# Moving the sums of squares of k and q in an attention stage from VectorE to ScalarE

## The chip, the cores and the metric

The kernel runs on one core of a Trainium2 chip. The metric is the device time of one execution in microseconds. The core's engines are called PE (TensorE), DVE (VectorE), ACT (ScalarE), POOL (GpSimd) and SP (SyncE, which here only issues DMAs). They run side by side and meet only at semaphores.

## The reference, cut to what matters

The kernel computes two layers, each an attention and a feed-forward part. The change concerns the second attention alone. There q and k are normalised per head before the scores:

```
def rms_norm(x, w):
    var = jnp.mean(jnp.square(x.astype(jnp.float32)), axis=-1, keepdims=True)
    return (x * jax.lax.rsqrt(var + EPS)).astype(x.dtype) * w
...
kv = jnp.concatenate([context, latents], axis=1)     # 64 + 256 keys
q, k, v = ...                                        # 32 heads of q, 8 of k and v, 128 wide
q = rms_norm(q, q_norm_w); k = rms_norm(k, k_norm_w)
scores = jnp.einsum('bhgqd,bhkd->bhgqk', qg, k) * scale
out = einsum(softmax(scores), v) @ Wo
```

The sum of squares over the 128 elements of a head is what moves to another engine.

## The kernel before, in words

The second attention (`attn1_phase`) runs 32 units: 8 groups g (a k/v head and its four q heads) times 4 batches b, so unit n = 4g + b. Group 0 and group 7 are written out, groups 1 to 6 are a hardware loop. Each engine has its own program (`body`), and its order is written out by hand. All matrix products are made of three passes over a high and a low part of each operand (`mm3`, lines 55 to 57): ACT copies a PSUM bank to the high part, DVE then subtracts to get the low part. Each unit is software-pipelined: while unit n makes its k, v, q and scores, the engines turn the probabilities of unit n-1 (`turn`, lines 1224 and 1229), multiply them with v (`p_v`, 1243), and project (`out`).

What one unit does, in the order of PE:

- k and v products (`kv`), and for even b also the context's (`cx`);
- turns j = 0 and 1 of unit n-1, the q product of token tile 0, whose last of four chunks waits for the low part of turn 0; turns 2 and 3 (turn 3 waits for the low part of turn 1), the q product of tile 1, turns 4 and 5 (turn 4 waits for the low part of turn 3);
- `p_v` of head pair 0; the transposes of k (L1314), which reuse the PSUM bank of turn 4 and so wait for its low part; the transposes of q, tile 0 (L1323), which wait likewise for turn 5; `p_v` of head pair 1; the transposes of q, tile 1, which wait for the low part of kT;
- scores 0 and 1, out 0, scores 2, out 1, scores 3.

What ACT does beside it: copies of k and v (L1142 to L1149), then for j = 0 to 5 the high part of turn j (`t_evac`, L1126 and L1129), with the copy of q tile 0 after j = 1 and of tile 1 after j = 3 (L1159), the high part of `p_v` 0 (`pv_evac`, L1134) after j = 5, then kT (L1163, L1166), qT (L1171), and the four pairs of exponentials (L1183, with row sums as accumulated outputs).

DVE makes the low parts (`t_lo` L962 and L966, `pv_lo` L972, kT_lo L1058, qT_lo L1068), the sums of squares of k (L1031: 3 for even b, 2 for odd) between the low parts of turns 0 and 1, those of q (`q_squares`, L986: four per tile) after the low parts of turns 3 and 5, the scaling of k (L1044), the row maxima and their scaled negatives (L993, L997), the reciprocals and scaling of p (L1003, L1008). POOL turns the sums of squares into reciprocal roots (rk L923 and L925, rq L931 and L933), scales a quarter of p (L916), and makes the low parts of the weights: of `o` in unit b = 1 right behind rk, of `kv` and `q` in unit b = 3 (L909, four or two pieces of 128x512). k cannot be turned before DVE has scaled it, and the exponentials need rq.

Of the kernel before, what the change touches and what calls it, by code (L numbers as in the profile page):

```python
# [23 lines left out]
ALU = mybir.AluOpType  # L24
# [8 lines left out]
HD = 128  # L33
NKV = 8
GH = 4
# [780 lines left out]
def attn1_phase(nc, k, sem, ln):  # L816


    def sems(*names):
        return [sem("a1_" + n) for n in names]  # L820
# [7 lines left out]
        "t_full", "t_hi", "t_split", "kt_full", "kt_hi", "kt_split", "qt_full", "qt_hi", "qt_split")  # L828
    ssk_ready, rk_ms, rk_ready, k_scaled, ssq_ready, rq_ms, rq_ready = sems(
# [61 lines left out]
    with nc.Block() as block:  # L891
# [60 lines left out]
        def _(dve):  # L952
# [29 lines left out]
            def q_squares(n, b, tile):  # L982
                dve.wait_ge(q_copied, 2 * n + tile + 1)
                for h in range(GH):
                    q = k.q_raw[:, tile, h * HD:(h + 1) * HD]
                    last = dve.tensor_tensor_reduce(k.dump[:, tile * GH + h, :], q, q, 1.0, 0.0, ALU.mult, ALU.add,  # L986
                                                    k.ssq[:, tile * GH + h:tile * GH + h + 1])
                if tile == 1:
                    last.then_inc(ssq_ready, 1)

# [21 lines left out]
            def body(g, first, nxt):  # L1012
                for b in range(BATCH):
# [16 lines left out]
                    for i in range(nk):  # L1030
                        last = dve.tensor_tensor_reduce(k.dump[:, 2 * GH + i, :], k.k_raw[:, i, :], k.k_raw[:, i, :], 1.0, 0.0,  # L1031
                                                        ALU.mult, ALU.add, k.ssk[:, i:i + 1])
                    last.then_inc(ssk_ready, 1)
# [15 lines left out]
                    q_squares(n, b, 0)  # L1049
# [3 lines left out]
                    q_squares(n, b, 1)  # L1053
# [62 lines left out]
            dve.wait_ge(stats_set, 1)  # L1116
# [3 lines left out]
        def _(act):  # L1120
# [15 lines left out]

            def body(g, first, nxt):
                for b in range(BATCH):
                    n, prev = BATCH * g + b, not (first and b == 0)
                    act.wait_ge(kv_full, n + 1)  # L1140
                    bank = y_bank(b, "kv")[:, :].rearrange("p (t n) -> p t n", t=2)
                    act.activation(k.k_raw[:, 0:2, :], bank[:, :, 0:HD], ACT.Copy)  # L1142
                    act.activation(k.v[0][:, b, 0:2, :], bank[:, :, HD:2 * HD], ACT.Copy).then_inc(kv_hi, 1)
                    if b % 2 == 0:
                        act.wait_ge(cx_full, 2 * g + b // 2 + 1)
                        act.activation(k.k_raw[:, 2, :], y_bank(b, "cx")[:, 0:HD], ACT.Copy)
# [4 lines left out]
                        last.then_inc(cx_hi, 1)  # L1151
                    for j in range(6):
                        if prev:
                            t_evac(n, b, j)
                            if j == 5:
                                pv_evac(n, b, 0)
                        if j in (1, 3):
                            act.wait_ge(q_full, 2 * n + j // 2 + 1)
                            act.activation(k.q_raw[:, j // 2, :], y_bank(b, "q", j // 2)[:, :], ACT.Copy)\  # L1159
                               .then_inc(q_copied, 1)  # L1160
                    act.wait_ge(kt_full, n + 1)
# [39 lines left out]

            loop(act, body, tail)
# [486 lines left out]
```

## Time and profile before

| | us |
|---|---|
| median of 3 runs | 1532.51 (1532.06 to 1532.99) |
| profiled execution | 1530.52 |
| its span | 1528.7 |
| PE busy | 1427.2 (93%) |
| DVE busy | 1136.9 (74%) |
| ACT busy | 756.8 (50%) |
| POOL busy | 519.6 (34%) |

The span is the time from the first to the last instruction of the profiled execution; 1.8 us lie around it. The first copy of k (L1142) starts at 583.9 us and the last at 1424.2, which places the second attention: it is some 58% of the span. The granted TensorE clock is full in all of it. Busy time of PE is modelled, because matmuls overlap: the start of one to the start of the next is the better measure.

### The profile page before, as it was taken

The page shows a single profiled execution, that of the slowest core. Times are in us where ns is not written, and L with a number is a line of the kernel's source. Part 1 is how long each engine was busy: PE and PEld are TensorE (multiplying, and loading weights), DVE is VectorE, ACT ScalarE, POOL GpSimd, SP SyncE. Part 2 cuts the span into 40 slices and gives each one's busy share as a digit, 9 for nine tenths or more (in the row PEclk, how much of TensorE's full clock was granted, in tenths as well). Part 3 has the DMA queues.
Part 4 walks back from the last instruction along what each step waited for, and adds up shares of the span by engine and source line. Part 5 has one row for each costly group of instructions (what it writes and reads, how often), then busy time and mean ns, then how long its engine had stood idle before and what let it go on. Part 6 is the DMA issues. An engine that isn't in the chain of part 4 may idle for free. (4 is left out here: it accounts for less than half of the span.)

```text
span 1528.7 us, 24378 instructions
## 1 busy us (share of the span) xinstructions
PE 1427.2 (93%) x8064; PEld 1209.9 (79%) x8064; DVE 1136.9 (74%) x2870; ACT 756.8 (50%) x2127; POOL 519.6 (34%) x586
## 2 busy tenths in 40 slices
PE   5999999999999998999999999999999999999879
PEld 4888888887778887787888878878878887877767
DVE  7888888888651426778778788787787787787765
ACT  5666666667220314545544545555545545455531
POOL 5733333443691822232132133132132223322220
PEclk9999999999999999999999999999999999999999
DMA  4111111220230400100101001001001001000001
GB/s 186 70 67 44 69 55 69 69 69 1 83 112 28 136 13 0 70 1 6 65 1 68 1 0 69 0 0 69 0 0 69 0 0 69 14 29 13 1 1 55
DMA packets 14933, 63.75 MB, mean 42 GB/s; under 512 B 1760, under 2 KB 1760, under 8 KB 10656
## 3 DMA queue, kind: packets, MB, share of 16 engines
q1 hardware_dynamic: 14880, 63.07, 11.6%
q8 instruction: 30, 0.49, 0.1%
q14 instruction: 23, 0.19, 0.0%
HBM read 60.97 MB, written 2.10 MB: 41 GB/s over the span
## 5 line engine op out<-in xcount | busy, mean ns | idle before, releaser
L1183 ACT ACTIVATE p<-psum,nb,rq 128x320 f32<-128x320 f32 x256 | 155.4, 614 | 208.4 <-DVE nb L997 208.3
L55 PE MATMUL psum<-w1q_hi,xnT_lo 128*128 128x512 f32 x256 | 107.8, 421 | 7.9 <-DVE v_lo L1017 4.3
L993 DVE TENSOR_REDUCE mx<-psum 128x2 f32<-128x640 f32 x128 | 105.0, 820 | 9.3 <-PE psum L57 3.8
L923 POOL TENSOR_TENSOR rk<-ssk,rms_eps 128x3 f32<-128x3 f32 x32 | 6.3, 196 | 299.7 <-DVE ssk L1031 299.7
L962 DVE TENSOR_TENSOR pT_lo<-psum,pT_hi 128x512 fp32r<-128x512 f32 x128 | 87.9, 687 | 23.4 <-ACT pT_hi L1126 21.4
L243 POOL TENSOR_TENSOR p<-p,rinv 128x256 f32<-128x256 f32 x64 | 39.3, 614 | 192.0 <-DVE rinv L319 192.0
L434 ACT ACTIVATE p<-psum,nb 128x64 f32<-128x64 f32 x256 | 76.8, 313 | 51.0 <-DVE nb L344 50.9
L57 PE MATMUL psum<-w1q_hi,xnT_hi 128*128 128x512 f32 x256 | 100.6, 393 | 0.0
L55 PE MATMUL psum<-w1o_hi,oT_lo 128*128 128x512 f32 x256 | 100.4, 392 | 0.0
L56 PE MATMUL psum<-w1o_lo,oT_hi 128*128 128x512 f32 x256 | 100.3, 392 | 0.0
L56 PE MATMUL psum<-w1q_lo,xnT_hi 128*128 128x512 f32 x256 | 99.8, 390 | 0.0
L57 PE MATMUL psum<-w1o_hi,oT_hi 128*128 128x512 f32 x256 | 99.8, 390 | 0.0
L313 DVE TENSOR_TENSOR VW_lo<-psum,VW_hi 64x512 fp32r<-64x512 f32 x128 | 88.0, 687 | 13.5 <-ACT VW_hi L419 11.6
L1159 ACT ACTIVATE q_raw<-psum 128x512 f32<-128x512 f32 x64 | 38.2, 598 | 117.6 <-PE psum L57 117.6
L1229 PE MATMUL psum<-ident,p 128*128 128x128 f32 x512 | 73.2, 276 | 21.8 <-DVE pT_lo L962 13.7
L419 ACT ACTIVATE VW_hi<-psum 64x512 fp32r<-64x512 f32 x128 | 75.8, 592 | 22.9 <-PE psum L57 21.4
L55 PE MATMUL psum<-kT_hi,qT_lo 128*128 128x320 f32 x256 | 83.4, 326 | 3.2 <-ACT p L1183 2.3
L55 PE MATMUL psum<-w_kv_hi,xnT_lo 128*128 128x256 f32 x288 | 82.3, 286 | 3.1 <-PEq L642 1.8
L1229 PEld LDWEIGHTS psum<-ident,p 128*128 128x128 f32 x512 | 57.6, 140 | 34.1 <-DVE pT_lo L962 17.7
L1008 DVE TENSOR_SCALAR p<-p,rinv 128x320 f32<-128x320 f32 x192 | 80.4, 461 | 3.4
L57 PE MATMUL psum<-w_kv_hi,xnT_hi 128*128 128x256 f32 x288 | 82.2, 285 | 0.0
L56 PE MATMUL psum<-w_kv_lo,xnT_hi 128*128 128x256 f32 x288 | 82.2, 285 | 0.0
(249 smaller groups left out, 4821.8 us busy)
## 6 DMA issues: line engine op xcount, KB each, us to landing
raw_q<-in_w0q SPq DMA_DIRECT2D x8, 1024.0 KB, 4.9
raw_o<-in_w0o SPq DMA_DIRECT2D x8, 1024.0 KB, 4.8
raw_q<-in_w1q SPq DMA_DIRECT2D x8, 1024.0 KB, 7.5
raw_o<-in_w1o SPq DMA_DIRECT2D x8, 1024.0 KB, 4.8
raw_kv<-in_w_gu SPq DMA_DIRECT2D x10, 512.0 KB, 3.5
raw_gu<-in_w_gu SPq DMA_DIRECT2D x10, 512.0 KB, 3.6
raw_kv<-in_w0kv SPq DMA_DIRECT2D x8, 515.0 KB, 3.3
raw_kv<-in_w1kv SPq DMA_DIRECT2D x8, 512.0 KB, 5.5
```

The costliest lines, as they stand in the source:

```text
L55: pe.matmul(out, w[1], m[0], start=start, stop=False)
L56: pe.matmul(out, w[0], m[1], start=False, stop=False)
L57: return pe.matmul(out, w[0], m[0], start=False, stop=stop)
L243: pool.tensor_tensor(p, p, spread(k.rinv0[:, t % 4, :]), ALU.mult).then_inc(p_ready, 1)
L313: last = dve.tensor_tensor(k.VW[1][r, h // 2, 2 * pr + bp, :], bank[64 * bp:64 * bp + 64, :], f(k.VW[0][r, h // 2, 2 * pr + bp, :]), ALU.s ...
L419: last = act.activation(k.VW[0][r, h // 2, 2 * pr + bp, :], bank[64 * bp:64 * bp + 64, :], ACT.Copy)
L434: last = act.activation(k.p0[:, s % 4, h * CTX:(h + 1) * CTX], s_bank[s % 2][:, h * CTX:(h + 1) * CTX], ACT.Exp, scale=SCALE, bias=k.nb0[: ...
L962: last = dve.tensor_tensor(k.pT[1][:, kt, 2 * hp:2 * hp + 2, :], bank.rearrange("p (h q) -> p h q", h=2), f(k.pT[0][:, kt, 2 * hp:2 * hp + ...
L993: dve.tensor_reduce(k.mx[:, stat(j)], s_pair(j), AX.X, ALU.max).then_inc(mx_ready, 1)
L1008: last = dve.tensor_scalar(k.p1[:, tile, h, :], k.p1[:, tile, h, :], k.rinv[:, tile * GH + h:tile * GH + h + 1], None, ALU.mult)
L1183: last = act.activation(k.p1[:, tile, h, :], s_pair(j)[:, h % 2, :], ACT.Exp, bias=k.nb[:, i:i + 1], scale=k.rq[:, i:i + 1], accum_out=k.r ...
L1229: last = pe.transpose(bank[:, (2 * hh + tile) * PART:(2 * hh + tile + 1) * PART], k.p1[:, tile, 2 * hp + hh, CTX * hh + kt * PART:CTX * hh ...
```

## The change

Both kinds of sums of squares leave DVE. ACT makes each by one square with an accumulated output into the same `ssk` and `ssq` columns. The squares of k come right behind the copies of k and v (and, in even units, of the context's), ahead of the high part of turn 0. The four of q tile 0 come between the high part of turn 3 and the copy of q tile 1; two of tile 1 right behind that copy, ahead of turn 4; the other two between turn 5 and `p_v` 0. A new semaphore tells ACT that its own copy of k is written; before the squares of q it waits on `q_copied` in the same way. The wait for the first memset of POOL moves from DVE to ACT.

```
--- before.py
+++ after.py
@@ -826,6 +826,7 @@
         "q_full", "q_copied", "pv_full", "pv_hi", "pv_split", "d_full", "x_added")
     t_full, t_hi, t_split, kt_full, kt_hi, kt_split, qt_full, qt_hi, qt_split = sems(
         "t_full", "t_hi", "t_split", "kt_full", "kt_hi", "kt_split", "qt_full", "qt_hi", "qt_split")
+    k_copied = sem("a1_k_copied")
     ssk_ready, rk_ms, rk_ready, k_scaled, ssq_ready, rq_ms, rq_ready = sems(
         "ssk", "rk_ms", "rk", "k_scaled", "ssq", "rq_ms", "rq")
     s_full, mx_ready, nb_ready, exp_done, rinv_ready, p_scaled, stats_set, p_scaled_pool = sems(
@@ -979,15 +980,6 @@
                 dve.scalar_tensor_tensor(out=k.x[:, t, :], in0=y_bank(b, "d", j)[:, :], scalar=k.gate[:, 1:2],
                                          in1=k.x[:, t, :], op0=ALU.mult, op1=ALU.add).then_inc(x_added, 1)
 
-            def q_squares(n, b, tile):
-                dve.wait_ge(q_copied, 2 * n + tile + 1)
-                for h in range(GH):
-                    q = k.q_raw[:, tile, h * HD:(h + 1) * HD]
-                    last = dve.tensor_tensor_reduce(k.dump[:, tile * GH + h, :], q, q, 1.0, 0.0, ALU.mult, ALU.add,
-                                                    k.ssq[:, tile * GH + h:tile * GH + h + 1])
-                if tile == 1:
-                    last.then_inc(ssq_ready, 1)
-
             def row_max(n, j):
                 dve.wait_ge(s_full, 4 * n + j + 1)
                 dve.tensor_reduce(k.mx[:, stat(j)], s_pair(j), AX.X, ALU.max).then_inc(mx_ready, 1)
@@ -1027,10 +1019,6 @@
                     if prev:
                         t_lo(n, b, 0)
                     nk = 3 if b % 2 == 0 else 2
-                    for i in range(nk):
-                        last = dve.tensor_tensor_reduce(k.dump[:, 2 * GH + i, :], k.k_raw[:, i, :], k.k_raw[:, i, :], 1.0, 0.0,
-                                                        ALU.mult, ALU.add, k.ssk[:, i:i + 1])
-                    last.then_inc(ssk_ready, 1)
                     if not nxt and b >= 2:
                         ln.dve_stats(dve, 3, 2 * b - 4)
                         ln.dve_stats(dve, 3, 2 * b - 3)
@@ -1046,11 +1034,9 @@
                     if prev:
                         t_lo(n, b, 2)
                         t_lo(n, b, 3)
-                    q_squares(n, b, 0)
                     if prev:
                         t_lo(n, b, 4)
                         t_lo(n, b, 5)
-                    q_squares(n, b, 1)
                     if prev:
                         pv_lo(n, b, 0)
                     dve.wait_ge(kt_hi, n + 1)
@@ -1113,7 +1099,6 @@
 
             w_hi("q", 0)
             own_lo("q")
-            dve.wait_ge(stats_set, 1)
             loop(dve, body, tail)
 
         @block.scalar
@@ -1134,30 +1119,56 @@
                 act.activation(k.oT[0][:, 2 * hp:2 * hp + 2, :],
                                y_bank(b, "pv", hp)[:, :].rearrange("p (h q) -> p h q", h=2), ACT.Copy).then_inc(pv_hi, 1)
 
+            def k_squares(n, nk):
+                act.wait_ge(k_copied, n + 1)
+                for i in range(nk):
+                    last = act.activation(k.dump[:, 2 * GH + i, :], k.k_raw[:, i, :], ACT.Square,
+                                          accum_out=k.ssk[:, i:i + 1])
+                last.then_inc(ssk_ready, 1)
+
+            def q_squares(n, tile, heads):
+                act.wait_ge(q_copied, 2 * n + tile + 1)
+                for h in heads:
+                    i = tile * GH + h
+                    last = act.activation(k.dump[:, i, :], k.q_raw[:, tile, h * HD:(h + 1) * HD], ACT.Square,
+                                          accum_out=k.ssq[:, i:i + 1])
+                if i == 2 * GH - 1:
+                    last.then_inc(ssq_ready, 1)
+
             def body(g, first, nxt):
                 for b in range(BATCH):
                     n, prev = BATCH * g + b, not (first and b == 0)
+                    nk = 3 if b % 2 == 0 else 2
                     act.wait_ge(kv_full, n + 1)
                     bank = y_bank(b, "kv")[:, :].rearrange("p (t n) -> p t n", t=2)
-                    act.activation(k.k_raw[:, 0:2, :], bank[:, :, 0:HD], ACT.Copy)
+                    last = act.activation(k.k_raw[:, 0:2, :], bank[:, :, 0:HD], ACT.Copy)
+                    if nk == 2:
+                        last.then_inc(k_copied, 1)
                     act.activation(k.v[0][:, b, 0:2, :], bank[:, :, HD:2 * HD], ACT.Copy).then_inc(kv_hi, 1)
                     if b % 2 == 0:
                         act.wait_ge(cx_full, 2 * g + b // 2 + 1)
-                        act.activation(k.k_raw[:, 2, :], y_bank(b, "cx")[:, 0:HD], ACT.Copy)
+                        act.activation(k.k_raw[:, 2, :], y_bank(b, "cx")[:, 0:HD], ACT.Copy).then_inc(k_copied, 1)
                         for i in range(2):
                             for half in (slice(0, 64), slice(64, PART)):
                                 last = act.activation(k.v[0][half, b + i, 2, :],
                                                       y_bank(b, "cx")[64 * i:64 * i + 64, HD:2 * HD], ACT.Copy)
                         last.then_inc(cx_hi, 1)
+                    k_squares(n, nk)
                     for j in range(6):
                         if prev:
                             t_evac(n, b, j)
-                            if j == 5:
-                                pv_evac(n, b, 0)
+                        if j == 3:
+                            q_squares(n, 0, range(GH))
                         if j in (1, 3):
                             act.wait_ge(q_full, 2 * n + j // 2 + 1)
                             act.activation(k.q_raw[:, j // 2, :], y_bank(b, "q", j // 2)[:, :], ACT.Copy)\
                                .then_inc(q_copied, 1)
+                        if j == 3:
+                            q_squares(n, 1, (0, 1))
+                        if j == 5:
+                            q_squares(n, 1, (2, 3))
+                            if prev:
+                                pv_evac(n, b, 0)
                     act.wait_ge(kt_full, n + 1)
                     bank = x_bank(b, "k")
                     last = act.activation(k.kT[0][:, b, CTX:KEYS], bank[:, 0:SEQ], ACT.Copy, scale=k.qkw[:, 0:1])
@@ -1199,6 +1210,7 @@
                 for t in (4, 5):
                     ln.act_hi(act, 3, t, ln_bank(4, t % 2))
 
+            act.wait_ge(stats_set, 1)
             loop(act, body, tail)
 
         @block.tensor
```

## Rows read from the trace of the kernel before

**Rows 1.** Busy time of each engine over four units, 850.26 to 958.89 us: sum and mean.
```profile
sum 108.63, PE 104.56 PEld 88.68 DVE 86.19 ACT 55.52 POOL 29.39; mean PE 26.14 PEld 22.17 DVE 21.55 ACT 13.88 POOL 7.35
```

**Rows 2.** One line's instructions: ns min/median/max, first and last start.
```profile
L986 DVE CUSTOM_DVE_ANT_0 dump<-q_raw x256: 279/285/1033, 590.7 to 1435.6; 128x128 f32<-128x128 f32 x128
```

**Rows 3.** ACT's groups by shape: out<-in, shapes, count | busy us, mean ns | idle before.
```profile
L1163 ACT ACTIVATE kT_hi<-psum,qkw 128x256 fp32r<-128x256 f32 x32 | 15.0, 468 | 0.0
L731 ACT ACTIVATE hT_hi<-f_h 128x512 fp32r<-128x512 f32 x20 | 12.7, 633 | 45.3 <-DVE f_h L705 45.3
L1142 ACT ACTIVATE k_raw<-psum 128x256 f32<-128x256 f32 x32 | 12.2, 382 | 25.2 <-PE psum L57 25.2
...
L444 ACT ACT_TABLE_LOAD x1 | 1.3, 1283 | 0.7 <-PEq L1679 0.7
```

**Rows 4.** Timeline of ACT, first attention: start us, us, instruction [idle before <-releaser].
```profile
202.16 0.30 ACT L434 ACTIVATE p<-psum,nb 128x64 f32<-128x64 f32 x1
...
202.45 0.31 ACT L434 ACTIVATE p<-psum,nb 128x64 f32<-128x64 f32 x1
```

**Rows 5.** Timeline of ACT, unit b=2 of a middle group.
```profile
853.00 1.08 ACT L1126 ACTIVATE pT_hi<-psum 128x512 fp32r<-128x512 f32 x2
...
859.66 0.60 ACT L1159 ACTIVATE q_raw<-psum 128x512 f32<-128x512 f32 x1 [1.81 <-PE psum L57]
860.15 0.59 ACT L1126 ACTIVATE pT_hi<-psum 128x512 fp32r<-128x512 f32 x1
```

**Rows 6.** Timeline of DVE, the same unit b=2.
```profile
854.24 0.69 DVE L962 TENSOR_TENSOR pT_lo<-psum,pT_hi 128x512 fp32r<-128x512 f32 x1
...
860.78 0.69 DVE L962 TENSOR_TENSOR pT_lo<-psum,pT_hi 128x512 fp32r<-128x512 f32 x1 [0.84 <-ACT pT_hi L1126]
```

**Rows 7.** Timeline of PE, the same unit b=2.
```profile
854.98 0.50 PE L55 MATMUL psum<-w1q_hi,xnT_lo 128*128 128x512 f32 x1 [0.38 <-DVE pT_lo L962]
...
862.42 0.66 PE L1323 MATMUL psum<-ident,q_raw 128*128 128x128 f32 x4
...
864.53 0.39 PE L1243 MATMUL psum<-pT_hi,v_hi 128*128 128x512 f32 x1
865.10 0.63 PE L1323 MATMUL psum<-ident,q_raw 128*128 128x128 f32 x4 [0.19 <-DVE kT_lo L1062]
865.79 0.41 PE L55 MATMUL psum<-kT_hi,qT_lo 128*128 128x320 f32 x1
```

**Rows 8.** Timeline of PE's weight loads, the same unit b=2.
```profile
856.22 0.42 PEld L1229 LDWEIGHTS psum<-ident,p 128*128 128x128 f32 x4 [0.29 <-DVE pT_lo L962]
```

**Rows 9.** Timeline of ACT, unit b=3 of the same group.
```profile
885.48 0.59 ACT L1126 ACTIVATE pT_hi<-psum 128x512 fp32r<-128x512 f32 x1
```

**Rows 10.** Timeline of PE, the same unit b=3.
```profile
887.74 0.66 PE L1323 MATMUL psum<-ident,q_raw 128*128 128x128 f32 x4
...
890.09 0.60 PE L1323 MATMUL psum<-ident,q_raw 128*128 128x128 f32 x4
890.60 0.41 PE L55 MATMUL psum<-kT_hi,qT_lo 128*128 128x320 f32 x1
```

**Rows 11.** Timeline of ACT, unit b=1 of the next group.
```profile
932.94 1.10 ACT L1126 ACTIVATE pT_hi<-psum 128x512 fp32r<-128x512 f32 x2
```

**Rows 12.** Timeline of POOL, the same unit b=1.
```profile
936.45 5.05 POOL L909 TENSOR_TENSOR w1o_lo<-raw_o,w1o_hi 128x512 fp32r<-128x512 f32 x4
```

**Rows 13.** Timeline of DVE, the same unit b=1.
```profile
936.52 2.58 DVE L1044 TENSOR_SCALAR k_raw<-k_raw,rk 128x128 f32<-128x128 f32 x2 [0.63 <-POOL rk L925]
```

**Rows 14.** Timeline of PE, the same unit b=1.
```profile
939.01 0.39 PE L57 MATMUL psum<-w1q_hi,xnT_hi 128*128 128x512 f32 x1
940.77 0.66 PE L1229 MATMUL psum<-ident,p 128*128 128x128 f32 x4 [1.37 <-DVE pT_lo L962]
...
943.85 0.66 PE L1323 MATMUL psum<-ident,q_raw 128*128 128x128 f32 x4
```

**Rows 15.** Timeline of ACT, the first unit of the stage.
```profile
591.50 0.47 ACT L1163 ACTIVATE kT_hi<-psum,qkw 128x256 fp32r<-128x256 f32 x1
```

More of the change, by code:

```diff
@@ L828, in attn1_phase @@
         "t_full", "t_hi", "t_split", "kt_full", "kt_hi", "kt_split", "qt_full", "qt_hi", "qt_split")
+    k_copied = sem("a1_k_copied")
     ssk_ready, rk_ms, rk_ready, k_scaled, ssq_ready, rq_ms, rq_ready = sems(
@@ L980, in x_add @@
                                          in1=k.x[:, t, :], op0=ALU.mult, op1=ALU.add).then_inc(x_added, 1)
[L982 to L989, printed above, removed]
             def row_max(n, j):
@@ L1029, in body @@
                     nk = 3 if b % 2 == 0 else 2
[L1030 to L1033, printed above, removed]
                     if not nxt and b >= 2:
@@ L1115, in _ @@
             own_lo("q")
-            dve.wait_ge(stats_set, 1)
             loop(dve, body, tail)
@@ L1135, in pv_evac, with k_squares, q_squares @@
                                y_bank(b, "pv", hp)[:, :].rearrange("p (h q) -> p h q", h=2), ACT.Copy).then_inc(pv_hi, 1)
+            def k_squares(n, nk):
+                act.wait_ge(k_copied, n + 1)
+                for i in range(nk):
+                    last = act.activation(k.dump[:, 2 * GH + i, :], k.k_raw[:, i, :], ACT.Square,
+                                          accum_out=k.ssk[:, i:i + 1])
+                last.then_inc(ssk_ready, 1)
+            def q_squares(n, tile, heads):
+                act.wait_ge(q_copied, 2 * n + tile + 1)
+                for h in heads:
+                    i = tile * GH + h
+                    last = act.activation(k.dump[:, i, :], k.q_raw[:, tile, h * HD:(h + 1) * HD], ACT.Square,
+                                          accum_out=k.ssq[:, i:i + 1])
+                if i == 2 * GH - 1:
+                    last.then_inc(ssq_ready, 1)
             def body(g, first, nxt):
@@ L1139, in body @@
                     n, prev = BATCH * g + b, not (first and b == 0)
+                    nk = 3 if b % 2 == 0 else 2
                     act.wait_ge(kv_full, n + 1)
                     bank = y_bank(b, "kv")[:, :].rearrange("p (t n) -> p t n", t=2)
-                    act.activation(k.k_raw[:, 0:2, :], bank[:, :, 0:HD], ACT.Copy)
+                    last = act.activation(k.k_raw[:, 0:2, :], bank[:, :, 0:HD], ACT.Copy)
+                    if nk == 2:
+                        last.then_inc(k_copied, 1)
                     act.activation(k.v[0][:, b, 0:2, :], bank[:, :, HD:2 * HD], ACT.Copy).then_inc(kv_hi, 1)
@@ L1145, in body @@
                         act.wait_ge(cx_full, 2 * g + b // 2 + 1)
-                        act.activation(k.k_raw[:, 2, :], y_bank(b, "cx")[:, 0:HD], ACT.Copy)
+                        act.activation(k.k_raw[:, 2, :], y_bank(b, "cx")[:, 0:HD], ACT.Copy).then_inc(k_copied, 1)
                         for i in range(2):
@@ L1151, in body @@
                         last.then_inc(cx_hi, 1)
+                    k_squares(n, nk)
                     for j in range(6):
@@ L1154, in body @@
                             t_evac(n, b, j)
-                            if j == 5:
-                                pv_evac(n, b, 0)
+                        if j == 3:
+                            q_squares(n, 0, range(GH))
                         if j in (1, 3):
@@ L1160, in body @@
                                .then_inc(q_copied, 1)
+                        if j == 3:
+                            q_squares(n, 1, (0, 1))
+                        if j == 5:
+                            q_squares(n, 1, (2, 3))
+                            if prev:
+                                pv_evac(n, b, 0)
                     act.wait_ge(kt_full, n + 1)
@@ L1200, in tail @@
                     ln.act_hi(act, 3, t, ln_bank(4, t % 2))
+            act.wait_ge(stats_set, 1)
             loop(act, body, tail)
```

2 lines of the change are left out of this document (removed).

## The prediction

> **What bounds the kernel now.** I read the windows first. In four units of the middle of the stage PE is busy 104.56 of 108.63 us, DVE 86.19, ACT 55.52 [rows 1]. So PE is the bound and everything else counts only where PE waits for it; a lighter DVE is worth nothing by itself. The timelines then show where PE waits, and the pattern repeats from group to group. In an even unit there are five places. The last chunk of the q product waits for the low part of turn 0 (0.38 us shown idle at 854.98) [rows 7]; turn 3 waits for that of turn 1 (0.29 on the weight loads) [rows 8]; the transposes of q tile 0 at 862.42 wait for turn 5; those of tile 1 at 865.10 wait for kT_lo; scores 0 at 865.79 wait for qT_lo [rows 7]. In unit b=1 there is one large wait: turn 4 starts at 940.77 instead of 939.24 (939.01 plus the 0.23 from one 512-column matmul to the next) because DVE is late with turn 3: 1.53 us [rows 14]. In b=3 the middle has only the wait of the q transposes for turn 5 [rows 10].
>
> The reader should see who sets the wait at turn 5. ACT starts the high part of turn 4 at 860.15, directly behind its copy of q tile 1 at 859.66 [rows 5]; DVE had been idle 0.84 us when it took that bank at 860.78 [rows 6]; PE gets the q transposes out at 862.42 [rows 7], 2.27 us after ACT's start. In b=3 the same distance is 885.48 to 887.74, 2.26 us [rows 9, 10]. So this point moves one to one with ACT's turn 4, and DVE's squares, which sit in DVE's idle time, do not matter for it. Two of the moved squares go exactly in front of it.
>
> **What goes.** 256 squares of q at a median of 0.285 us [rows 2] and 80 of k of the same form leave DVE, about 96 us of busy records, less in elapsed time because they overlap. Nearly all of it lies beside waits for ACT or POOL, so I cost the removal at nothing except in b=1 (below). The cover is DVE's own idle time, 0.84 us in row 860.78 alone [rows 6]; if it were gone, less DVE work could only help.
>
> **The price of a square on ACT.** No square with accumulation is in the trace. The nearest rows are the exponentials 128x64 with an accumulated output and one pointer operand: 0.29 us from start to start [rows 4]. Copies of 128x512 and 128x256 take 0.60 and 0.382 us [rows 3, 5], so 64 more columns cost 0.054. A pointer operand costs 0.468 - 0.382 = 0.086 [rows 3], and the square has none. A source in SBUF costs 0.633 - 0.60 = 0.033 more [rows 3, 5]. That gives 0.29 + 0.054 - 0.086 + 0.033 = 0.29 us each. Lower end 0.24 (the source free and a little less), upper end 0.40 (a pointer for the bias after all). I take 0.29, since the exponential differs from it only by terms that rows show. The wait of ACT for its own copy of q is new too: the copy is 0.60 long [rows 5], where the next instruction used to start after 0.49. I take 0.05 for the semaphore, between 0 and 0.15: 0.65 - 0.49 = 0.16 us.
>
> **Squares of k.** Three in an even unit move the high part of turn 0 from 853.00 to 853.87 [rows 5]. DVE needs 0.63 from there (860.15 to 860.78 [rows 5, 6]), so turn 0's low part starts at 854.50 instead of 854.24 [rows 6]: PE's wait grows by 0.26. Without DVE's three squares the low part of turn 1 comes directly behind, and the 0.29 at turn 3 goes: net -0.03. In odd units two squares cost 0.58, which by the same steps stays under PE's need: the low part of turn 0 is about 0.3 us early there. Nothing.
>
> **Squares of q.** Four of tile 0 (1.16 us) go into ACT's idle 1.81 before the copy of tile 1 [rows 5]: nothing, with 0.65 left, about 0.4 after the turns that now run later. Two of tile 1 and the wait, 0.58 + 0.16 = 0.74 us, push turn 4. Even unit: q transposes +0.74 - 0.03 = +0.71. Behind them p_v 1 now covers what tile 1 waited for: 865.10 less (864.53 + 0.23) = 0.34 [rows 7]. Scores 0 used to follow after 0.69 against 0.51 in b=3 [rows 7, 10]: 0.18 more. Net 0.71 - 0.34 - 0.18 = +0.19. In b=3 nothing waits behind the q transposes, so +0.74. The last two squares (0.58, ahead of p_v 0's high part) delay kT, but kT_lo is still some 0.3 us before PE's need, because DVE no longer makes its four squares in front of it. ssq is ready no later than before within about 0.3 us, and POOL's rq has over 2 us until the first exponential: nothing.
>
> **Unit b=1.** DVE's scaling of k takes 2.58 us for two small instructions, beside POOL's 5.05 us of w1o_lo that started 0.07 us earlier [rows 12, 13]; each scaling ends with a piece of POOL's (1.26 us). Behind it stands turn 3's low part, hence the 1.53. With the change ACT makes the k squares from 932.94 [rows 11], so rk is ready near 934.8 instead of 936.5. DVE reaches the scaling 0.63 (its wait for rk) and 0.43 (two squares) earlier, at 935.46. POOL has then already started at 934.8 and its pieces end near 936.0 and 937.3, so the second scaling ends near 937.4 instead of 939.1, and turn 3's low part 1.7 us earlier: the 1.53 goes whole. But then ACT's own order is the next thing late: the copy of q tile 1 at 939.43, plus 0.65 and 0.58, puts turn 4 at 940.66, and 2.27 later, at 942.93, come the q transposes instead of 943.85 [rows 14]. Net -0.92.
>
> What the Trainium skill says here (SBUF — State Buffer, section "SBUF: two separate sides"): DVE in a two-port mode and GpSimd take turns on one shared port pair, held for a whole instruction, while ACT never waits for anyone. The 2.58 us agrees. By that rule the earlier start of POOL doesn't free the scaling, it only moves both; with the lock gone the scaling would end a further 1.5 us earlier, which changes nothing, since ACT's turn 4 is then last.
>
> **First unit.** There kT starts at 591.50 directly behind the q copy [rows 15], and PE waits for it. Four squares and the wait go between: 4 x 0.29 + 0.16 = +1.3 us, once.
>
> **The sum.** 15 even units with a predecessor x 0.19 = 2.9; 8 units b=3 x 0.74 = 5.9; 8 units b=1 x -0.92 = -7.4; first unit 1.3. Total +2.7 us. On the profiled execution's 1530.5 that is 1533.2; that one execution is 2.0 below the median of the runs, and on the median 1532.5 it is 1535.2. A measurement of this kernel can tell 0.2%, 3.1 us, from no change, so the forecast lies just inside "same". A change of 0.01 in the price of a square is worth 1.1 us in all (5 squares in series in 15 units, 2 in 16, 4 once). Prices of 0.26 to 0.33 give -0.6 to +7.1, so 1531.9 to 1539.6.
>
> **The rivals.**
> - *Slower: b=1 gains nothing.* If the scaling of k is still held past 939 (POOL's pieces start 1.7 us earlier, but DVE loses the port to one piece more, 1.26 us, and turn 3 is then 1.1 us late again), the -7.4 goes and the sum is +10: 1542.6, from 1540 to 1546. Against it: DVE needs only two turns between pieces.
> - *Slower: the square is dear.* At 0.40 or more the k squares lengthen PE's wait in even units by 0.6, and turn 4 shifts by 0.96 or more: +2.7 + 11 x 1.11 = +15: 1547. For it: nobody made a square here. It decides from 0.30 on.
> - *Faster: the square is cheap.* At 0.24, and with no wait of ACT for its own copy, turn 4 shifts by 0.48 only. Then even units give -0.22 (q wait 0.48 less 0.34 and 0.18, k squares -0.18), b=3 0.48, b=1 -1.18, the first unit 1.0: -7.9, 1524.6; halfway to that is 1529. Delays of b=3 that its later waits on DVE swallow would work the same way.
> - *Table switches.* The one table load of the trace is 1.283 us [rows 3]. Were square and exponential in different tables, a load ahead of the k squares and a load ahead of the exponentials would fall in every unit; the first stands before turn 0 and costs PE about 1.2 us: +37, 1570. The Trainium skill (ScalarE: Activation LUTs, "Table sets: the hidden batching unit") names relu, copy, identity and abs as being in every set and puts a switch at about 2.7 us with its drain, which would give over 80 us; square is not in that list. The one load for exponential, tanh and copy together in the trace is the only sign for a wide set.
> - *It does nothing*: ACT's squares all fall in idle time that I read as too short: 1532.5.
>
> **Chances.** Forecast 0.50 (0.29 inside 0.2%, 0.21 above it), b=1 without gain 0.13, dear square 0.11, cheap square 0.20, tables 0.03, nothing 0.03. Hence faster 0.20, same 0.32, slower 0.48. The signs are split, so the forecast's own 1531.9 to 1539.6 stands beside the wide range, 1528 to 1546, which leaves out the tables, the worst of the dear square and the far half of the cheap one.
>
> **What would show it.** Right: squares at 0.29 from start to start; q transposes 2.27 us behind ACT's turn 4 with turn 4 0.7 later against the q copy; turn 4 of b=1 on time; a group's 108.6 us now about 109. Wrong: the scaling of k in b=1 ending after 938.3 on this scale, a second table load, squares above 0.33, or the wait of PE for turn 5 unmoved although ACT's turn 4 is later.

## The result, and the profile after

| | before | after |
|---|---|---|
| median | 1532.75 us (4 runs, 1532.06 to 1534.02) | 1549.09 us (4 runs, 1547.60 to 1551.40) |
| ratio | | 1.0106 [1.0090, 1.0122] |
| profiled execution | 1530.52 | 1547.60 |
| its span | 1528.7 | 1545.8 |
| DVE busy | 1136.9 | 1052.5 |
| ACT busy | 756.8 | 863.1 |

Slower by 1.1%, 16.3 us on the medians and 17.1 between the two profiled executions. The forecast was 1535.2 with a range to 1546: the sign was the one with most chance, the size was missed, and the measured time lies outside the range. The 17.1 us compare one execution of each kernel, and part of them is not the change's, as the last steps below show.

Rows of the page of after, the kernel with the change: busy time by engine, a group of DVE and one of PE (busy us, mean ns | idle before, releaser) and the DMA queue that carries instructions.

```profile
PE 1430.0 (93%) x8064; PEld 1211.1 (78%) x8064; DVE 1052.5 (68%) x2198; ACT 863.1 (56%) x2799; POOL 520.7 (34%) x586
...
L963 DVE TENSOR_TENSOR pT_lo<-psum,pT_hi 128x512 fp32r<-128x512 f32 x128 | 85.5, 688 | 86.7 <-ACT pT_hi L1111 85.7
...
L55 PE MATMUL psum<-w1q_hi,xnT_lo 128*128 128x512 f32 x256 | 109.3, 427 | 19.2 <-DVE v_lo L1009 10.2
...
q14 instruction: 48, 0.39, 0.1%
```

84 us left DVE and 106 came to ACT. DVE did not get faster, it waits: 86.7 us ahead of the low parts, where before has 23.4. The last two rows hold the part that I had not seen: PE waits 10.2 us for v_lo (4.3 in before), and the instruction queue carried 48 packets where before had 23. In the groups of ACT by shape the change also shows a new kind of idle time, 6.5 us that end in "issue", which means that the engine waited for nothing that the profile shows:

```profile
L1144 ACT ACTIVATE k_raw<-psum 128x256 f32<-128x256 f32 x32 | 12.3, 384 | 31.7 <-PE psum L57 25.2 <-issue 6.5
...
L444 ACT ACT_TABLE_LOAD x1 | 1.3, 1283 | 0.7 <-PEq L1691 0.7
```

To place the 17.1 us I took PE's timeline and measured each unit from its first k/v matmul to that of the next. Units in the hardware loop (groups 2 to 5 of before; for after the first pass, group 1, apart from groups 2 to 6, which are entered by the loop's jump, the branch from its end back to its first instruction):

| us | b=0 | b=1 | b=2 | b=3 | group |
|---|---|---|---|---|---|
| before | 29.07 | 26.5 | 27.7 | 25.32 | 108.6 |
| after, first pass of the loop | 29.65 | 25.41 | 28.31 | 26.05 | 109.42 |
| after, entered by the loop's jump | 31.11 to 31.71 | 25.37 | 28.31 | 26.05 | 110.9 to 111.5 |

The sum of the difference: first group 0.43, first pass 0.73, the five later passes 12.70, last group 0.11, ahead of the stage 0.43 (its first matmul is at 579.72 instead of 579.30), behind the start of the last unit 2.7 (110.34 to the end instead of 107.63). That is 17.1. (Most of the 2.7 turns out below not to be the change's.) Of the 12.70, the five jumps are 157.2 - 5 x 29.65 = 8.9: the b=0 units after a jump against the one that is entered without.

ACT of after at such a jump (start us, us, instruction [idle before <-releaser]):

```profile
909.38 0.61 ACT L1194 ACTIVATE p<-psum,nb,rq 128x320 f32<-128x320 f32 x1
909.89 0.20 ACT L1194 ACTIVATION_READ_ACCUMULATOR p<-psum,nb,rq 128x1 f32 x1
911.43 0.39 ACT L1144 ACTIVATE k_raw<-psum 128x256 f32<-128x256 f32 x1 [1.35 <-issue]
```

and PE behind it:

```profile
908.84 0.28 PE L57 MATMUL psum<-w_kv_hi,ctxT_hi 128*128 128x256 f32 x1
909.67 1.09 PE L1241 MATMUL psum<-ident,p 128*128 128x128 f32 x8 [0.55 <-DVE p L1000]
912.60 0.50 PE L55 MATMUL psum<-w1q_hi,xnT_lo 128*128 128x512 f32 x1 [1.84 <-DVE v_lo L1009]
...
915.67 0.50 PE L55 MATMUL psum<-w1q_hi,xnT_lo 128*128 128x512 f32 x1 [0.73 <-DVE pT_lo L963]
```

k and v were in PSUM from 909.1 on, but ACT issues nothing between 910.09 and 911.43, and nothing in the profile holds it. Its last exponential belongs to one pass of the loop, its first copy to the next. The releaser named for PE, v_lo of DVE, is only the messenger: it waits for ACT's v_hi. The branch record of ACT's sequencer lies at 908.84 and its next record at 911.34, 2.50 us later, and one packet of the instruction queue falls in between (909.78 to 910.27). In before the same two records are 0.24 us apart with no packet between them, the copy of k follows the last exponential at once, and PE's wait at this place is 0.63:

```profile
905.45 0.20 ACT L1183 ACTIVATION_READ_ACCUMULATOR p<-psum,nb,rq 128x1 f32 x1
905.54 0.38 ACT L1142 ACTIVATE k_raw<-psum 128x256 f32<-128x256 f32 x1
```

```profile
906.95 0.50 PE L55 MATMUL psum<-w1q_hi,xnT_lo 128*128 128x512 f32 x1 [0.63 <-DVE v_lo L1017]
```

Two stretches of after (us, busy of PE, PEld, DVE, ACT, POOL, granted clock, DMA share, GB/s). The first shows what follows PE's stall at the first, third and fifth jump; the second lies behind the last unit and is needed below:

```profile
1024.10:1027.50 3.40, 3.40 (x10) 2.66 (x9) 2.92 (x9) 2.05 (x8) 1.04 (x2) 0.51 0.01 2
1468.00:1475.00 7.00, 5.81 (x19) 4.19 (x20) 3.30 (x7) 1.76 (x5) 1.20 (x4) 0.53 0.00 0
```

The granted clock in the first is 0.51, the lower of TensorE's two levels (1.2 GHz), for 3.4 us. Jumps with it give units of 31.6 to 31.7, those without 31.1: 0.55 us each, three times, inside the 8.9.

### The profile page after: what moved, and what is told of

Same layout as the page of the kernel before. It is cut to its first block and busy times, and to the rows that moved or that the text cites. A ratio compares the mean times of both kernels' runs of the same rounds, so it can differ in the third digit from the quotient of the medians.

```text
span 1545.8 us, 24378 instructions
## 1 busy us (share of the span) xinstructions
PE 1430.0 (93%) x8064; PEld 1211.1 (78%) x8064; DVE 1052.5 (68%) x2198; ACT 863.1 (56%) x2799; POOL 520.7 (34%) x586
## 5 line engine op out<-in xcount | busy, mean ns | idle before, releaser
L963 DVE TENSOR_TENSOR pT_lo<-psum,pT_hi 128x512 fp32r<-128x512 f32 x128 | 85.5, 688 | 86.7 <-ACT pT_hi L1111 85.7
L55 PE MATMUL psum<-w1q_hi,xnT_lo 128*128 128x512 f32 x256 | 109.3, 427 | 19.2 <-DVE v_lo L1009 10.2
L917 POOL TENSOR_TENSOR p<-p,rinv 128x640 f32<-128x640 f32 x32 | 40.1, 1254 | 139.4 <-DVE rinv L995 139.4
L57 PE MATMUL psum<-kT_hi,qT_hi 128*128 128x320 f32 x256 | 79.1, 309 | 0.0
```

The costliest lines, as they stand in the source:

```text
L55: pe.matmul(out, w[1], m[0], start=start, stop=False)
L57: return pe.matmul(out, w[0], m[0], start=False, stop=stop)
L917: pool.tensor_tensor(p, p, k.rinv[:, stat(j)].unsqueeze(2).to_broadcast([PART, 2, KEYS]), ALU.mult).then_inc(p_scaled_pool, 1)
L963: last = dve.tensor_tensor(k.pT[1][:, kt, 2 * hp:2 * hp + 2, :], bank.rearrange("p (h q) -> p h q", h=2), f(k.pT[0][:, kt, 2 * hp:2 * hp + ...
```

## The experiments

The theory after the result: two things are added, the squares in ACT's order (some 0.8 us a group), and a price of the loop's jump on ACT (1.5 to 2.1 us a group). The rival for the second: squares at the head of the unit delay v_hi or the low parts in b=0. The first kernels below separate these.

**ACT's loop written out.** `e1_act_unrolled` is after with the passes of ACT's program written one behind the other, and nothing else:

```
-            loop(act, body, tail)
+            body(0, True, True)
+            for g in range(1, NKV - 1):
+                body(g, False, True)
+            body(NKV - 1, False, False)
+            tail(NKV * BATCH)
```

> The changed kernel, but with the 8 groups of ACT's program written out one after the other instead of groups 1 to 6 as a hardware loop. Theory A (the loop edge): with the squares ACT's loop body holds 288 recorded instructions per turn instead of 204, it no longer stays resident, and each jump back waits for code: 2.4 us from the branch to the next instruction instead of 0.24, five times, and PE loses 1.5 to 2.1 us each time with a short fall of its clock. Then this kernel has no 1.35 us of idle ACT at a group's start and runs about 9 us faster than the changed kernel, near 1540 (ratio to before 1.005). Theory B (the order and load of ACT alone): the gap comes from the new waits or from ACT's fuller queue; writing the loop out changes nothing, 1549 (1.0106).

Measured 1540.13, ratio 1.0038 [1.0024, 1.0052]. All six groups are now 109.3 to 109.4, b=0 is 29.65 each time. The copy of k stands right behind the last exponential:

```profile
907.53 0.20 ACT L1194 ACTIVATION_READ_ACCUMULATOR p<-psum,nb,rq 128x1 f32 x1
907.63 0.38 ACT L1144 ACTIVATE k_raw<-psum 128x256 f32<-128x256 f32 x1
```

So 9.0 us of the loss (1549.09 - 1540.13) were the jump. The order of ACT's instructions is the same, so squares at the head of the unit are not its cause.

`e2_before_act_unrolled` is the same edit on before.

> The kernel before, with ACT's groups written out. A control: both theories expect no change beyond 2 us (1531 to 1534), since its jump back took only 0.24 us. If it is faster by more, writing out has a value of its own that has to be taken off the verdict on the changed kernel.

Measured 1532.36, 0.9996 [0.9987, 1.0006], groups of 108.7 as in before. Before's jump was free; writing out a loop is worth nothing by itself.

**Length without work.** `e3_before_padded` gives ACT's loop of before as many more instructions as the squares and their accumulator reads add (84 a pass), as one-column copies in idle time:

```
+            def pads(at, m):
+                for i in range(at, at + m):
+                    act.activation(k.pad[:, i:i + 1], k.qkw[:, 0:1], ACT.Copy)
...
                     if j in (1, 3):
+                            pads(5 * (j // 3), 5)
...
+                        if j in (0, 3):
+                            pads(10 + 5 * (j // 3), 5 + j // 3)
```

> The kernel before, its squares still on DVE, with 21 one-column copies per unit added on ACT (84 per turn of the loop, as many instructions as the squares and their accumulator reads bring), placed where ACT idles: 5 ahead of each copy of q, 5 ahead of the first exponentials and 6 ahead of the last. About 0.1 us each, so 0.5 us in waits of 1.8 us or more. Theory A: the gap at the jump back appears (2.4 us from the branch), about +9 us, near 1541. Theory B: no gap, within 2 us of before.

Measured 1543.27, 1.0055 [1.0038, 1.0071]. The other three units keep 26.5, 27.75 and 25.33; b=0 is 30.5 to 32.6. The gap is there though no square is:

```profile
910.19 0.20 ACT L1191 ACTIVATION_READ_ACCUMULATOR p<-psum,nb,rq 128x1 f32 x1
911.67 0.38 ACT L1147 ACTIVATE k_raw<-psum 128x256 f32<-128x256 f32 x1 [1.28 <-issue]
```

**Half of the change.** `e4_k_only` leaves the squares of q on DVE as in before and moves those of k. ACT's loop then has 224 records a pass, between the 204 of before and the 288 of after.

> The same as the kernel with the k squares alone on ACT, but with ACT's loop kept: one look at the loop edge with 20 instructions more per turn than before (224 against 204) and 64 fewer than in the change. If the time of the jump depends on how much code a turn holds, it is 0.24 us here, as before; if any growth breaks it, it is 2.4 us.

Measured 1540.75, in a single run. ACT's jump cost nothing any more, but the gap had moved to DVE, whose loop had become *shorter* (289 records a pass in the trace instead of 309):

```profile
905.42 0.68 DVE L1009 TENSOR_SCALAR p<-p,rinv 128x320 f32<-128x320 f32 x2
908.63 0.42 DVE L1018 TENSOR_TENSOR v_lo<-psum,v_hi 128x256 fp32r<-128x256 f32 x1 [2.52 <-issue]
908.97 0.27 DVE L1024 TENSOR_TENSOR v_lo<-psum,v_hi 64x128 fp32r<-64x128 f32 x1
911.16 0.90 DVE L1024 TENSOR_TENSOR v_lo<-psum,v_hi 64x128 fp32r<-64x128 f32 x3 [1.92 <-issue]
```

`e8_k_only_unrolled` is the same with ACT written out, so that no jump of ACT is in it. Both were put on record together, when only ACT's loop was suspected.

> Only the squares of k on ACT, ahead of turn 0 as in the change; those of q stay on DVE; ACT's groups written out, so that no loop edge is in it. My terms: even units +0.13 (turn 0 later, the wait at turn 3 gone), b=3 0.0, and b=1 gains the whole 1.53 and a little more, -1.7, because nothing on ACT is in front of turn 4. A group is 1.4 us shorter, in all about -11: 1522. Rival: the gain of b=1 comes from DVE's relief by the q squares too; then b=1 gains under 1.2 and the time is 1526 or more.

Measured 1540.71, 1.0055 [1.0037, 1.0073]: a miss of 19 us. Writing out ACT could not help, since DVE's jump was the one that cost: b=0 is 32.3 to 33.6 with a jump (to 33.9 in e4) and 29.2 without, b=1 24.96, b=2 27.88, b=3 25.33. So "a longer loop is dearer" was wrong as a rule. What then decides?

**The place of the loop.** I counted the engine's records in the trace, its sequencer's included, up to the loop's first instruction. The loop of the first attention is counted once, not six times, so that the number stands for a place in the program:

| kernel, engine | records ahead of the loop | records a pass | jump |
|---|---|---|---|
| before, ACT | 594 | 204 | free |
| after, ACT | 679 | 288 | gap |
| e3, ACT | 678 | 288 | gap |
| before, DVE | 719 | 309 | free |
| e4 and e8, DVE | 698 | 289 | gap |

A loop of 309 runs free while one of 289 that starts 21 earlier does not. If the place matters, moving the same loop by some instructions must remove the gap. `e10_shifted` is after with 32 one-column copies ahead of ACT's loop:

```
+        for i in range(32):
+            act.activation(k.pad[:, i:i + 1], k.qkw[:, 0:1], ACT.Copy)
         act.wait_ge(stats_set, 1)
         loop(act, body, tail)
```

> The changed kernel, loop kept, with 32 one-column copies on ACT ahead of its first unit, where ACT waits 13 us for PE anyway. Each turn of the loop stays exactly as long (288 recorded instructions); only the place where it begins in ACT's program moves by 32. Theory P (place): code is fetched in pieces of 8192 bytes on queue 14, and a loop jumps back without waiting if it touches few enough pieces; whether it does hangs on where it begins. The traces so far fit three pieces of 128 instructions: the changed kernel's loop would begin some 97 to 108 instructions into a piece and touch four, and 32 further on it begins near 1 to 12 and touches three. Then the jump takes 0.24 us, queue 14 carries 20 packets fewer and the time is that of the written-out kernel, about 1540. Theory S (size): ACT's loop stays resident only below some size between 224 and 288 instructions; then nothing changes, 1549.

Measured 1540.11, 1.0049 [1.0030, 1.0068], with its before at 1530.84. Groups are 109.4, the same as with the loop written out, and the instruction queue is back at before's count. The loop of 288 now begins at record 711. (Its first unit is 1.2 us longer than that of after, for a reason of its own that comes below.)

```profile
909.66 0.20 ACT L1195 ACTIVATION_READ_ACCUMULATOR p<-psum,nb,rq 128x1 f32 x1
909.75 0.38 ACT L1145 ACTIVATE k_raw<-psum 128x256 f32<-128x256 f32 x1
```

```profile
q14 instruction: 23, 0.19, 0.0%
```

`e11_k_only_shifted` does it for DVE's loop of e4: the same 32 copies (`dve.tensor_copy`) ahead of `loop(dve, ...)`.

> The kernel with the k squares alone on ACT and all loops kept, with 32 one-column copies on DVE ahead of its first unit. In the kernel without them it was DVE's jump that took 2.8 to 3.0 us, though DVE's loop had become shorter (289 recorded instructions against 309 before, where it took 0.3). Theory P: it began 107 to 127 into a piece and now begins 11 to 31 into one: the jump is back at 0.3 us, b=0 units fall from 32 to 34 us to 29.2, and the time is what I expected of this part from the start, about 1522 to 1524, plus up to 2 us for the copies. Theory S can't explain the longer jump of a shorter loop; under any theory in which the place doesn't matter the time stays at 1540.

Measured 1523.01, 0.9946 [0.9929, 0.9963]: 17.7 us below e4 and e8 by 32 instructions that compute nothing; DVE's loop of 289 begins at record 730 instead of 698. Its units are 29.2, 24.96, 27.86, 25.32. The squares of k alone are thus a gain, and it comes from b=1.

The Trainium skill (Runtime: NRT & Kernel Launch, section "Instruction fetch mechanics") states the mechanism: the instruction memory holds two blocks and is filled ahead in order, and "a taken branch whose target isn't in the current 2-page window forces a DMA fetch of the target page". The trace agrees in kind: in after five packets of the instruction queue fall in each pass of the loop, in before none from 771 to 1335 us. It also agrees that the place decides: an estimate by the page's block of 256 instructions is that a loop of 288 touches two blocks or three, depending on where it starts, and that 32 more ahead of it can make the difference. The packets in the traces are of 8192 bytes, where the page has blocks of 16 KiB. Which size sets the window, these runs can't tell; both fit the table, if each engine has one constant offset between its records and its place in memory.

**The squares of q alone.** `e9_q_only_unrolled` puts the squares of k back on DVE, with ACT's loop written out.

> Only the squares of q on ACT, where the change has them; those of k stay on DVE; ACT's groups written out. My terms: b=3 +0.73, even units +0.45, b=1 about 0 (its 1.53 of waiting for turn 3 stays, and ACT's squares are hidden in it). A group is 1.6 us longer, +12: 1546. Rival: the q squares are harmless and the loss of the even units comes from the k squares; then b=3 is unchanged and the time is 1534.

Measured 1544.36, 1.0075 [1.0057, 1.0093], near the 1546 expected. Units 29.49, 26.19, 28.16, 26.07: the whole +0.74 of b=3 and +0.4 of each even unit come from the squares of q, and b=1 gains only 0.3 by them.

**Other places for the squares.** The position of the q squares of tile 1 ahead of turn 4 was my named cause for b=3. `e12_q_behind_turn5` is e1 with all four behind turn 5:

```
-                        if j == 3:
-                            q_squares(n, 1, (0, 1))
                         if j == 5:
-                            q_squares(n, 1, (2, 3))
+                            q_squares(n, 1, range(GH))
```

> The changed kernel with ACT's groups written out, and with the two squares of q that stood between the copy of q tile 1 and turn 4 moved behind turn 5, to the other two. It takes those two squares and ACT's wait for its own copy out of the path of turn 4, and nothing else. My step: b=3 back to 25.3 us (from 26.05), b=1 to about 24.9 (from 25.37), even units 0.3 less than 28.31, so a group some 1.6 us shorter than the written-out kernel's 109.4, and about 12 us faster than its 1540: 1527. Rival: the delay of kT by four squares in a row costs as much as that of turn 4 did; then it stays within 3 us of 1540.

Measured 1525.02, 0.9956 [0.9941, 0.9971]. b=3 is back at 25.33, b=1 falls to 24.85. Even units fall only from 28.31 to 28.15 (b=2) and stay 0.4 above before. The squares of k ahead of turn 0 explain the smaller part: the q transposes of tile 0 come 0.15 later in the unit than in before. The other 0.3 is the rival of the expectation in small: four squares in a row stand ahead of kT, and PE waits for its low part at the transposes of tile 1 (0.19 in before [rows 7]):

```profile
862.35 0.63 PE L1337 MATMUL psum<-ident,q_raw 128*128 128x128 f32 x4 [0.47 <-DVE kT_lo L1048]
```

In b=3, where k has no context part, the same four squares cost nothing.

`e6_placed` moves both: the squares of k behind turn 1, the four of q tile 1 behind the high part of qT of tile 0, loop kept.

```
-                    k_squares(n, nk)
...
+                        if j == 1:
+                            k_squares(n, nk)
...
+                        if tile == 0:
+                            q_squares(n, 1, range(GH))
```

> The changed kernel, loop kept, with the squares in other places: those of k behind the high part of turn 1 instead of ahead of turn 0, and all four of q tile 1 behind qT of tile 0 instead of around turns 4 and 5. The high parts of turns 0, 4 and 5 are then as early as before. Theory A with my terms for the order: the loop edge still costs some 9 us, but even units and b=3 lose nothing (even ones may gain 0.3) and b=1 gains 0.8, so about 1533 to 1538. Theory B (load of ACT as such): it stays above 1545. If rq comes too late for the first exponentials, every unit grows by some tenths instead.

Measured 1529.01, 0.9955 [0.9939, 0.9971], 4 us under the fast end of what was expected, and still with the jump's price (b=0 31.15, but 28.56 in the first pass). `e7_placed_unrolled` takes the jump away too.

> The placement of the kernel with the squares in idle places, with ACT's groups written out as well. If the loop edge and the placement are separate terms, they add: units of b=0 28.5, b=1 25.5, b=2 27.2, b=3 25.3 us, a group 106.5 us against 108.6 before, and the time falls 14 to 18 us below before, 1516 to 1520. If the written-out program only helps where ACT is otherwise late, the gain over the looped placement is under 5 us, near 1525.

Measured 1515.12, 0.9884 [0.9867, 0.9902]: units 28.53, 25.5, 27.19, 25.31. The even units are 0.5 shorter than in before: PE begins the turns behind the q product of tile 0 as in before, but 0.28 goes at turn 3, where DVE no longer has squares ahead of turn 1's low part, and 0.27 more ahead of the q transposes of tile 1. The jump alone was 13.9 us between e6 and e7.

`e13_placed_k_early` is e7 with the two squares of k of odd units back ahead of turn 0, where they were free:

```
+                    if nk == 2:
+                        k_squares(n, nk)
...
-                        if j == 1:
+                        if j == 1 and nk == 3:
                             k_squares(n, nk)
```

> The fastest kernel so far (squares placed in idle time, ACT's groups written out, 1515) with the k squares of odd units back ahead of turn 0, those of even units behind turn 1. In odd units the low part of turn 0 has about 0.3 us to spare, so b=3 stays at 25.3 us, and b=1 loses the 0.86 us that turn 4 still waits there: 25.5 to about 24.7. Eight such units: 5 to 6 us faster, near 1509. If POOL's port is what holds k in b=1 whatever the start, b=1 stays at 25.5 and the time at 1515.

Measured 1510.02, 0.9855 [0.9839, 0.9872], the fastest kernel of the study: b=1 24.65, group 105.67 against 108.6. In 620 to 1400 us PE's busy time is 761.34 of 780; before has 750.11 in the same window. The row of e13, in the order of the two stretches above:

```profile
620.00:1400.00 780.00, 761.34 (x4380) 653.34 (x4379) 557.43 (x1193) 494.28 (x1690) 215.74 (x225) 1.00 0.06 25
```

So the move itself was a good one. It lost by its places in ACT's order and by where the loop came to lie.

## Why the prediction was wrong, step by step

**The missing term: the loop's edge.** I costed 336 more squares on ACT by their time on the engine and gave the loop's own edge no term, neither in the sum nor in a rival. It cost 8.9 us in the profiled execution, over three times the net +2.7 of my whole sum. This is the step that failed; the mis-sized even unit comes second. The lighter DVE has the same risk, as e4 showed. Nothing in before's rows could give the price, since its jumps were free, but it should have stood among the unknowns with a bound: the Trainium skill's page above says that a jump back can wait for code, and the edit changes the length of two engines' loops. Put right by this term alone, 1535.2 becomes 1544.1.

**The even unit: +0.19 predicted, +0.58 measured.** Unit b=2 of after, ACT, DVE and PE.

```profile
856.70 0.29 ACT L1125 ACTIVATE dump<-k_raw 128x128 f32<-128x128 f32 x1
856.90 0.19 ACT L1125 ACTIVATION_READ_ACCUMULATOR dump<-k_raw 128x1 f32 x1
857.11 1.09 ACT L1111 ACTIVATE pT_hi<-psum 128x512 fp32r<-128x512 f32 x2
...
862.92 0.60 ACT L1164 ACTIVATE q_raw<-psum 128x512 f32<-128x512 f32 x1 [0.38 <-PE psum L57]
863.55 0.31 ACT L1133 ACTIVATE dump<-q_raw 128x128 f32<-128x128 f32 x1
863.77 0.19 ACT L1133 ACTIVATION_READ_ACCUMULATOR dump<-q_raw 128x1 f32 x1
863.86 0.29 ACT L1133 ACTIVATE dump<-q_raw 128x128 f32<-128x128 f32 x1
864.06 0.19 ACT L1133 ACTIVATION_READ_ACCUMULATOR dump<-q_raw 128x1 f32 x1
864.16 0.58 ACT L1111 ACTIVATE pT_hi<-psum 128x512 fp32r<-128x512 f32 x1
```

```profile
857.74 1.29 DVE L963 TENSOR_TENSOR pT_lo<-psum,pT_hi 128x512 fp32r<-128x512 f32 x2 [0.44 <-ACT pT_hi L1111]
...
864.76 0.69 DVE L963 TENSOR_TENSOR pT_lo<-psum,pT_hi 128x512 fp32r<-128x512 f32 x1 [2.40 <-ACT pT_hi L1111]
```

```profile
858.49 0.50 PE L55 MATMUL psum<-w1q_hi,xnT_lo 128*128 128x512 f32 x1 [0.78 <-DVE pT_lo L963]
...
866.40 0.66 PE L1335 MATMUL psum<-ident,q_raw 128*128 128x128 f32 x4 [0.34 <-DVE pT_hi L967]
...
868.80 0.63 PE L1335 MATMUL psum<-ident,q_raw 128*128 128x128 f32 x4
869.49 0.41 PE L55 MATMUL psum<-kT_hi,qT_lo 128*128 128x320 f32 x1
```

- *Price of a square, 0.29: right.* The rows of the timeline give 0.30 from start to start (863.55 to 863.86 to 864.16), 0.31 and 0.29 long. The wait for ACT's own copy is 863.55 - 862.92 = 0.63, where I had 0.65. Turn 4's high part starts 1.24 after the copy of q instead of 0.49 [rows 5]: +0.75, predicted +0.74.
- *Squares of k, -0.03: wrong.* The wait at turn 0 grew by 0.40 (0.38 [rows 7] to 0.78), not 0.26: behind the last of the three squares turn 0 starts 0.41 later, not 0.29. That turn 3's wait goes was right (0.28 back). Net +0.13; e11, with these squares alone, has it too (even units +0.13 and +0.16).
- *From ACT's turn 4 to the q transposes 2.27 us: right*, 2.24 (864.16 to 866.40).
- *What later waits absorb, 0.52: wrong.* The q transposes come 0.88 later against the unit's start (16.12 us after it instead of 15.24, means of four groups), those of tile 1 0.59 later (0.34 expected to go, 0.29 went), and the scores also 0.59 later. The 0.18 between transposes and scores was to go as in b=3, but it stayed: 0.69 here, 0.69 in before [rows 7]. Everything that feeds qT came later with the transposes. 0.19 + 0.16 + 0.05 + 0.18 = 0.58.

15 such units: 8.7 us instead of 2.9, so this mis-sized term is 5.8 us.

**b=3: +0.74 predicted, +0.73 measured**, by the named cause: e12 takes it away whole.

**b=1: -0.92 predicted, -1.12 measured.** The scaling of k beside POOL:

```profile
941.34 5.08 POOL L910 TENSOR_TENSOR w1o_lo<-raw_o,w1o_hi 128x512 fp32r<-128x512 f32 x4
```

```profile
941.84 2.15 DVE L1032 TENSOR_SCALAR k_raw<-k_raw,rk 128x128 f32<-128x128 f32 x2
```

It is still held (2.15 us for two small instructions against 2.58 [rows 13]) but ends 8.2 us after the unit's start instead of 9.8 (8.1 predicted), and turn 4 starts on time. The q transposes come 0.94 sooner, near the 0.92; another 0.17 goes before the scores. e11 shows the cause apart: with the k squares alone b=1 is 24.95, a gain of 1.55, just the 1.53 that I read at [rows 14]; the q squares then take 0.4 back.

**First unit: +1.3 predicted, +0.33 measured.** The delay is there: scores begin 16.25 us after the unit's start instead of 15.05. But in before they ran at the lower clock, and in after at full; the clock of before is thus not full in all of the stage, as I had written ahead of the prediction. The windows of before and then of after:

```profile
594.00:597.40 3.40, 3.40 (x15) 3.27 (x14) 1.85 (x4) 0.97 (x2) 1.22 (x1) 0.50 0.00 0
```

```profile
594.00:597.40 3.40, 2.03 (x14) 1.88 (x15) 2.33 (x6) 2.63 (x5) 1.32 (x1) 1.00 0.00 0
```

e2 has the order of before, and its granted clock is 1.00 in these 3.4 us: its first unit takes 21.02 us, and that of after 22.22. At equal clock the squares thus cost 1.20, so this term was right, and it was the clock that hid it: the lower one made before's first unit 0.87 longer (21.89 against e2's 21.02) and e10's 1.19 longer (23.41 against 22.22). Which of the two clocks comes didn't follow from anything I know how to read.

**Behind the last unit: nothing predicted, +2.7 measured, and mostly not by the change.** The second of the two stretches above lies there: the granted clock is 0.53 over 7 us, and over the whole tail 0.94 instead of 0.97. But kernels without a square on ACT have it too: from the start of the last unit to the end it takes 107.6 us in before, 110.1 in e2 and e3, 109.7 to 109.8 with the k squares alone (e4, e8, e11), and 109.3 to 112.1 in the others. Before's own profiled execution is the short one, and e2, whose tail is 2.4 us longer, measures the same as before in the medians (ratio 0.9996), while before's own 15 executions beside it reach from 1530.01 to 1534.62. So most of the 2.7 is, as far as these runs show, a difference between executions. What sets the clock there stays open.

**The rivals.** The dear square came nearest in time, 1547, by a mechanism that isn't there (0.30, not 0.40). The cheap square is false by the same rows (and halfway to it was 1529.9, not the 1529 that I wrote: I had mixed the profiled execution with the median). Table switches are false: the one table load of the trace of after is that of before, shown above, and square, exponential and tanh run under it. "b=1 gains nothing" and "it does nothing" are false. With a jump that costs nothing the kernel is e1 or e10, 1540.1, inside the wide range, though just above the forecast's own 1539.6.

## What to carry to other kernels

An edit that changes how many instructions an engine has in a hardware loop, or ahead of it, can put a price on every jump back (1.4 to 4.7 us of the unit behind it in the runs here), on the engine that gained instructions or on the one that lost them; look for idle time that ends in "issue" at the loop's first instruction and for packets of the instruction queue inside the loop, and cure it by writing the loop out or by shifting it. Work that moves to an idle engine is not free by that engine's busy share: it costs what the next hand-over behind it is late, so it goes behind the evacuations that PE waits for, here behind turn 1 and behind the high part of qT of tile 0. Behind turn 5 was too early in even units, where kT is next. And a saving that one unit shows behind a wait (0.18 before the scores) may only be counted in another when its own inputs did not move too.

## What the runs showed of the hardware

- The same hardware loop, begun 32 instructions later, had no gap at its jump or one of 1.35 us on ACT, and on DVE none or two of 2.52 and 1.92 us. A shorter loop had a dearer jump than a longer one.
- A square of 128x128 with accumulation takes 0.29 to 0.30 from start to start on ACT, its accumulator read included. The next plain instruction started 0.30 after the last square in some places and 0.41 in others (863.86 to 864.16, 856.70 to 857.11); what decides is open.
- PE stalled 1.75 to 1.84 us at the five jumps of after. The first, third and fifth stall (1.80, 1.77, 1.75) were followed by 3.4 us at half the granted clock; the two longest (1.84, 1.82) were not. In e6 all five stalls, 1.94 to 2.04, were.
- Before and e2 differ only in ACT's loop being written out, and measure the same in the medians. The mean granted clock over the last 108 and 110 us of their profiled executions was 0.97 and 0.92, and that stretch took 2.4 us longer in the second.
